# Moving a row normalisation from ScalarE to VectorE in a planned MLP, attention and MLP kernel, with new planner numbers

## The reference, cut to what matters

```
x = x + 0.5 * ffn(layernorm(x))     # pass 0
x = x + attn(layernorm(x))          # pass 1 (projections), pass 2 (output projection)
x = x + 0.5 * ffn(layernorm(x))     # pass 3
layernorm(x) = (x - mean) / sqrt(var + eps)
ffn:  fp4-quantise rows by blocks of 16 -> gate, up (704 wide) -> silu(gate) * up
      -> fp4-quantise -> down (256 wide)
attn: q, k, v projections; rms norm and rotary on q, k; 16 half-heads, causal softmax;
      difference of the two halves with lambda; layer norm per head; output projection
```

## Time and profile before

| | us |
|---|---|
| three runs, median | 2178.94 |
| three runs, lowest and highest | 2178.08 to 2182.39 |
| the profiled execution, device time | 2177.42 |
| its span, first to last instruction | 2175.7 |
| mean granted TensorE clock, share of full | 0.975 |

### The profile page before, as it was taken

The page is one execution under the profiler, slowest core; times in us unless marked ns, Lnnn a source line. Parts: engine busy times, 40 slices in busy tenths (PEclk is TensorE's granted clock), DMA queues, the critical chain, the costliest instruction groups (busy, mean ns, idle before and its releaser), DMA issues. The chain is left out here.

```text
span 2175.7 us, 39394 instructions
## 1 busy us (share of the span) xinstructions
PE 1884.4 (87%) x13634; PEld 782.7 (36%) x13634; DVE 1566.9 (72%) x3324; ACT 1710.4 (79%) x2531; POOL 1365.6 (63%) x1439
## 2 busy tenths in 40 slices
PE   2677998898998988998899899899998889999966
PEld 1333433343432433343332343343432333432223
DVE  7898888677826878887743998888864678741365
ACT  3456787977889888878889898778888889789952
POOL 7797776566724776886743686866853667630255
PEclk9899999999999999999999999999999999999987
DMA  4134544324211444334221445232441343320013
GB/s 124 31 60 79 88 72 85 51 63 86 42 40 27 84 84 94 68 70 84 47 52 20 69 78 89 59 91 49 64 70 37 62 81 68 74 47 1 11 33 69
DMA packets 477493, 136.16 MB, mean 63 GB/s; under 512 B 458224, under 2 KB 477040, under 8 KB 477296
## 3 DMA queue, kind: packets, MB, share of 16 engines
q1 hardware_dynamic: 477296, 133.65, 33.0%
HBM read 11.96 MB, written 8.39 MB: 9 GB/s over the span
## 5 line engine op out<-in xcount | busy, mean ns | idle before, releaser
L1048 ACT ACTIVATE probs<-psum 128x1024 f32<-128x1024 f32 (+3 forms) x1280 | 1066.9, 922 | 94.6 <-PE psum L1333 79.3
L1351 PE MATMUL psum_o<-probs,v_sb 128*32 128x512 f32 (+3 forms) x5120 | 570.5, 542 | 20.0 <-POOL probs L954 7.8
L1296 PE MATMUL psum<-w_gu_T,xT 128*128 128x512 f16 (+1 forms) x2304 | 510.8, 371 | 60.9 <-DMA xT<-x 14.6
L1333 PE MATMUL psum<-q_stack,k_stack 64*128 64x512 f16 (+3 forms) x2560 | 388.3, 353 | 84.4 <-ACT probs L1048 65.5
L1296 PEld LDWEIGHTS psum<-w_gu_T,xT 128*128 128x128 f16 x2304 | 213.7, 99 | 330.1 <-issue 50.1
L954 POOL TENSOR_SCALAR_AFFINE_SELECT probs<-probs 128x512 f32<-128x512 f32 x256 | 180.0, 709 | 237.4 <-ACT probs L1048 236.3
L1309 PE MATMUL psum<-w_down_T,hT 128*128 128x256 f16 x2176 | 267.8, 279 | 41.1 <-DMA hT<-h 19.7
L1333 PEld LDWEIGHTS psum<-q_stack,k_stack 64*128 64x128 f16 x2560 | 99.5, 93 | 503.6 <-ACT probs L1048 396.7
L921 POOL TENSOR_TENSOR hq<-grid,qscale 128x704 f32<-128x704 f32 x128 | 179.6, 1404 | 113.8 <-DVE grid L1147 113.8
L928 POOL TENSOR_TENSOR h<-hq,h 128x704 f16<-128x704 f32 x128 | 203.2, 1587 | 73.8 <-ACT h L1004 73.5
L1309 PEld LDWEIGHTS psum<-w_down_T,hT 128*128 128x128 f16 x2176 | 208.7, 100 | 106.7 <-issue 36.5
(11 more groups left out here) (120 smaller groups left out, 2294.6 us busy)
## 6 DMA issues: line engine op xcount, KB each, us to landing
xb<-L_attn_x SPq DMA_DIRECT2D x16, 512.0 KB, 3.9
out<-xb SPq DMA_DIRECT2D x16, 512.0 KB, 3.0
xT<-x SPq DMA_TRANSPOSE x128, 3.1
hT<-h SPq DMA_TRANSPOSE x128, 3.5
k_stack<-st SPq DMA_TRANSPOSE x64, 3.3
q_stack<-st SPq DMA_TRANSPOSE x64, 3.3
k_stack<-L_ffn_w_down SPq DMA_DIRECT2D x1, 704.0 KB, 4.0
k_stack<-L_ffn_w_gate SPq DMA_DIRECT2D x1, 512.0 KB, 5.1
```

Source lines behind the costliest of these rows:

```text
L1048: nc.scalar.activation(probs[:, s % 3, 2 * u:2 * u + 2, q0:CHUNK], psum[:, plan.pairs[s, u]:plan.pairs[s, u] + 2, q0:CHUNK], ACT.Exp, scal ...
L1296: last = nc.tensor.matmul(bank(e)[:, 0:hi - lo], xs[:, x, t % 2, k, :], w_gu_T[:, w, k, lo:hi], start=n == 0, stop=n == len(parts) - 1)
L1333: last = nc.tensor.matmul(psum[:, plan.pairs[s, u] + j, q0:CHUNK], k_stack[half, at, h, kt % NTC * P:(kt % NTC + 1) * P], q_stack[half, c ...
L1351: last = nc.tensor.matmul(psum_o[at:at + VD, q0:CHUNK], v_sb[:, kt // NTC % SLOTS * NTC + kt % NTC, 2 * g + u, :], probs[:, s % 3, 2 * u + ...
```

## The change

The normalisation stage `norm_a` is issued by DVE: one `tensor_scalar` for each tile computes `(x - mean) * rstd` with mean and `rstd` as scalars per partition. ACT no longer has the stage. POOL's `rstd` ends with `rstd` itself; the two instructions for `offset`, the tile and two semaphores are gone. In the hand-placed beginning DVE runs `norm_a` right before `scale_x`, and ACT runs nothing between its second and third weight square. The planner's tables change: `COST`, `REACH`, `DRAIN` and landing times, a new `LATE` and `AFTER` for hand-over times of single pairs of stages, `EARLY` for a bank that comes free before its stage ends, and the time that issuing a transposing DMA holds SP. `DUE` has new values in all its families and `WIDE` another selection. The diff, without the numbers of `DUE` and some declarations:

```
-WIDE = {0: (2, 3, 4, 8, 13, 14, 15), 1: (3, 7, 11, 12, 14, 15), 2: (1, 3, 4, 5, 7, 11, 14, 15), 3: (0, 2, 3, 4, 6, 7, 11, 14, 15)}
+WIDE = {0: (1, 5, 8, 9, 10, 12, 13, 14, 15), 1: (0, 1, 2, 3, 5, 6, 7, 13, 14, 15), 2: (3, 6, 8, 9, 11, 13, 14, 15), 3: (1, 5, 7, 10, 11, 13, 14, 15)}
-LANDING = 4000
+LANDING = 3400
...
-COST = dict(load=100, store=100, add_down=460, add_out=470, copy_o=670, dequant_h=1380, dequant_x=1060, divide_h=1390,
-            divide_x=1060, down=1970, gate=720, grid_h=890, grid_x=680, head_stats=2750, heads_out=2080, head_sum=460, square_o=400,
-            hidden=1380, high_h=800, high_qk=1160, high_x=640, low_h=1520, low_qk=1160, low_x=1160,
-            mask=630, norm_a=1090, norm_heads=690, norm_qk=680, points_h=890, points_x=690,
-            project_out=690, project_qk=1360, project_v=690, quant_h=1650, read_qk=690,
-            read_v=480, rms=4050, rope=1930, rope_add=1270, rstd=3340, scale_x=1290, square_h=790,
-            square_x=620, stats=1820, tanh=700, transpose_o=590, turn_x=200, turn_h=200, turn_qk=200)
+COST = dict(load=700, store=700, add_down=475, add_out=475, copy_o=680, dequant_h=1385, dequant_x=1058, divide_h=1385,
+            divide_x=1056, down=1860, gate=690, grid_h=890, grid_x=685, head_stats=2870, heads_out=2010, head_sum=460, square_o=400,
+            hidden=1300, high_h=790, high_qk=1150, high_x=625, low_h=1522, low_qk=1158, low_x=1156,
+            mask=640, norm_a=540, norm_heads=690, norm_qk=685, points_h=890, points_x=690,
+            project_out=650, project_qk=1300, project_v=650, quant_h=1650, read_qk=690,
+            read_v=470, rms=4170, rope=1940, rope_add=1270, rstd=2780, scale_x=1295, square_h=795,
+            square_x=620, stats=1820, tanh=690, transpose_o=470, turn_x=1250, turn_h=1400, turn_qk=2700)
 OVERLAP = dict(tensor=0, vector=80, scalar=100, gpsimd=40, sync=0)
-REACH = dict(tensor=140, vector=40, scalar=40, gpsimd=80, sync=100)
+REACH = dict(tensor=60, vector=40, scalar=40, gpsimd=80, sync=100)
 RELEASE = 60
-DRAIN = 140
+DRAIN = 170
+LATE = {("rstd", "norm_a"): 55, ("high_qk", "low_qk"): 60, ("copy_o", "transpose_o"): 85, ("scores", "exp"): 60}
+AFTER = {("grid_h", "points_h"): 35, ("grid_x", "points_x"): 35, ("gate", "gate"): 100, ("gate", "quant_h"): 100,
+         ("add_out", "stats"): 90, ("add_down", "stats"): 90, ("head_sum", "head_stats"): 90,
+         ("head_stats", "norm_heads"): 35, ("rope", "rms"): 35, ("norm_a", "scale_x"): 35}
+EARLY = dict(quant_h=460, scale_x=390)
...
-            dequant_h=0, low_h=0, rope_add=0, low_qk=0, mask=0)
+            dequant_h=0, low_h=0, rope_add=0, low_qk=0, mask=0, norm_a=0)
-TURNED_X, TURNED_H = 3300, 4200
+TURNED_X, TURNED_H, TURNED_QK = 2200, 2400, 2200
...
+        def lag(m, n):
+            of, to = self.stages[m][0], self.stages[n][0]
+            pair = m[0], n[0]
+            return REACH[to] + LATE.get(pair, 0) if of != to else AFTER.get(pair)
...
-                    met[n] = max(end[m] + REACH[self.stages[n][0]] if self.stages[m][0] != self.stages[n][0] else
-                                 left[m] for m in self.stages[n][3])
+                    met[n] = max(left[m] if lag(m, n) is None else end[m] + lag(m, n) for m in self.stages[n][3])
...
-                    loans[loan] = free_bank[b] = end[name] + REACH["tensor"]
+                    loans[loan] = free_bank[b] = end[name] + REACH["tensor"] - EARLY.get(name[0], 0)
...
-            add(norm, "scalar", at("norm_a"), needs, takes, frees)
+            add(norm, "vector", at("norm_a"), needs, takes, frees)
...
-                add(norm, "scalar", of_pair("norm_a", *pair), [("rstd", 1, c), ("norm_heads", "x", 2, NTC * (c - 2) // 2 - 1) if c >= 3 else None],
+                add(norm, "vector", of_pair("norm_a", *pair), [("rstd", 1, c), ("norm_heads", "x", 2, NTC * (c - 2) // 2 - 1) if c >= 3 else None],
...
-                [], [("st", t)], lands=LANDING)
+                [], [("st", t)], lands=TURNED_QK)
...
-                    [("scores", (s, u))], weight=230 * full // CHUNK)
+                    [("scores", (s, u))], weight=4 + 215 * full // CHUNK)
...
-                    weight=170 + 855 * full // CHUNK)
+                    weight=150 + 855 * full // CHUNK)
...
-                [("psum_o", (c, g))], [("probs", s)], weight=900 * full // CHUNK)
+                [("psum_o", (c, g))], [("probs", s)], weight=25 + 860 * full // CHUNK)
...
-                    n, o = EARLY_RSTD[e], offset[:, slot, :]
-                    nc.gpsimd.tensor_scalar(o, mean_var[:, slot, :, 0], -1.0, None, ALU.mult)\
-                        .then_inc(mean_negated, 1)
-                    nc.gpsimd.tensor_tensor(rstd[:, slot, :], t, y, ALU.mult).then_inc(early_rstd, 1)
-                    pool.wait_ge(mean_negated, n + 1)
-                    pool.wait_ge(early_rstd, n + 1)
-                    nc.gpsimd.tensor_tensor(o, o, rstd[:, slot, :], ALU.mult).then_inc(rstd_ready, 1)
+                    nc.gpsimd.tensor_tensor(rstd[:, slot, :], t, y, ALU.mult).then_inc(rstd_ready, 1)
...
-                elif e[0] == "norm_a":
...
-                    act.wait_ge(rstd_ready, RSTD["rstd", pas, 2 * p // NTC] + 1)
-                    for j in range(2):
-                        t = 2 * p + j
-                        i = t % NTC
-                        last = nc.scalar.activation(a[:, j * C:(j + 1) * C], xb[:, t % XB, :], ACT.Identity,
-                                                    bias=offset[:, slot, i:i + 1], scale=rstd[:, slot, i:i + 1])
-                    last.then_inc(early_normed, 1)
...
+                elif e[0] == "norm_a":
...
+                    before = last_low("x", (pas, p))
+                    if before:
+                        dve.wait_ge(low_ready, before)
+                    dve.wait_ge(rstd_ready, RSTD["rstd", pas, 2 * p // NTC] + 1)
+                    for j in range(2):
+                        t = 2 * p + j
+                        i = t % NTC
+                        last = nc.vector.tensor_scalar(a[:, j * C:(j + 1) * C], xb[:, t % XB, :],
+                                                       mean_var[:, slot, i, 0:1], rstd[:, slot, i:i + 1],
+                                                       ALU.subtract, ALU.mult)
+                    last.then_inc(early_normed, 1)
...
-                    vector_stages(dve, first["scale_x"])
+                    vector_stages(dve, first["norm_a"] + first["scale_x"])
...
-                        if i == 2:
-                            scalar_stages(act, first["norm_a"])
```

More of the change, by code:

```diff
@@ new lines @@
+    "quant_h3": (1257700, 128329, -1198020, -1930392, -197546, -2299546, -263471, 155916, 2507493, 4447889, -819760, -668114, -238246, 1056057, 2572883, 58971, 2588350, 2016998, 3140457, 1006166, -1192775, -432802, 3693548, 2754134, 3822575, 5763425, 6796468, 3720783, 5866866, 9472418, 2713345, 6331789),
+    "read_qk": (-2275201, -1665241, 46619, 1209385, -486133, 28992, -1106356, 346919, -1856335, -806712, 3076828, 3141783, 2439936, 4170447, 1363555, 1134917, 1057196, 2240352, 4011510, 4859110, 3179162, 5012717, 395203, 2114656, 2012872, 4693511, 650673, 2763797, -978070, 633382, 2104505, 3508172),
@@ new lines @@
+    "read_v": (-1738083, 193962, 648071, 1421781, 968234, 378105, 227935, 1835047, 1238024, 2157734, 688980, 1032469, 3935987, 6100348, -1588094, -177118, 1648812, 3826205, 2259728, 4995974, 2003981, 2282527, -359172, 2828252, 302645, 2071181, 1519232, 3276594, 2212377, 3332822, 632515, 2142383),
+    "rms": (-1424270, 382061, -1056880, 242518, 1329166, 1655857, -427873, 383003, 1198440, 2019739, -108322, -65278, 4240380, 5265659, -1848729, -1525625, 2689322, 4127738, 1532729, 3294075, 3363210, 4343741, -1217088, -61745, 3413416, 4800902, 219235, 2263829, -545703, 676159, -674618, 345017),
@@ L636, in macaron_kernel @@
         root_t = sb("root_t", [P, NTC])
-        offset = sb("offset", [P, STATS, NTC])
         minus_half = sb("minus_half", [P, NTC])
@@ L730, in macaron_kernel @@
         QUANT = ordinals(order["vector"], ("quant_h", "scale_x"))
-        EARLY_NORM = ordinals(order["scalar"], ("norm_a",))
-        EARLY_RSTD = ordinals(order["gpsimd"], ("rstd",))
+        EARLY_NORM = ordinals(order["vector"], ("norm_a",))
         DIVIDE = ordinals(order["gpsimd"], ("divide_x", "divide_h"))
@@ L978, in scalar_stages @@
                         .then_inc(full(e)[0] if e[1] == "x" else square_done, 1)
-                elif e[0] == "norm_a":
-                    pas, p = e[2:]
-                    slot = STAT[pas, 2 * p // NTC] % STATS
-                    a = buffers("x", (pas, p))[0]
-                    before = last_low("x", (pas, p))
-                    if before:
-                        act.wait_ge(low_ready, before)
-                    act.wait_ge(rstd_ready, RSTD["rstd", pas, 2 * p // NTC] + 1)
-                    for j in range(2):
-                        t = 2 * p + j
-                        i = t % NTC
```

(9 more changed lines are left out.)

61 lines of the change are left out of this document (28 added, 33 removed), and 136 rows, old and new, of the table DUE.

## The result

The changed kernel takes 2159.86 us in the median (2157.39 to 2161.51, 4 runs) against 2178.51 (2171.99 to 2182.39) for the kernel before, measured beside it: ratio 0.9916, 95% interval 0.989 to 0.9943. It is faster by 0.84%, about 19 us; forecast were 73. The range of 2050 to 2186 held the time, the forecast's own range of 2075 to 2145 did not.

A forecast was written before the change was run, and what follows sets the result against it. The kernel was taken to be bound by hand-overs between nearly balanced engines. Terms of -52, -2, -1.7, +13 and -30 us summed to -73, from 2177.4 to 2104.7, predicted as a 2106 us median; range 2050 to 2186, 8 in 10.

The forecast's parts named there:

- the worth of ACT's relief, -52 us: ACT loses norm_a: 139 us of its time come free, worth 0.37 each on the path; range 24 to 104 us.
- VectorE's side, +13 us: DVE gains 86 us of norms and holds, less 59.2 us of waits; net 27, costing in 11 of 22 stretches.
- The first rival: Each of 192 DVE norms is held by POOL through the shared port, 0.5 us each; slower, 2198 us; chance 0.12.
- a mean over 0.6 us speaks for the port: Sign in the norms' group on DVE: a mean this long would support the first rival; expected median was near 278 ns.
- The order's term, -30 us: New order from corrected transposing-DMA times removes a quarter of 122 us of transfer and loading waits; range 0 to 61.
- the 122 us of DMA waits of the prediction: Waits before the change: 76.6 us for transposing transfers in five entries, plus 45.4 us of DVE waiting for loaded rows.
- POOL's -2: POOL loses the offset's two instructions, 23.6 us of busy time; with 1 of the chain's 13, worth 2 us.
- the setup's -1.7: In the setup POOL's weight scaling can begin up to 1.65 us earlier, counted as 1.7 us.
- everything counts: Rival: ACT is nearly always last, its 104 us come off in full; 2040 to 2075 us; chance 0.14.
- PE is the bound: Rival: PE at about 90% needs that time, ACT's time is hidden; terms -24, +13, -4, -5; 2159 us; chance 0.22.
- if PE's waits for exps don't fall below 345 us and the time falls, the order did it: Sign on PE's waits for exps, 396.7 us before: it credits any gain to the new order.
- The sign of being wrong: Prediction wrong if PE's idle time doesn't shrink by about 70 us, or DVE's rstd waits grow past 30.8 us.

The follow-up runs named there:

- the second order: New table, norm left on ScalarE, due times from a search carried on for 40 minutes more, against the kernel before: 0.9831 (2138.49 us).
- the first refit: New table, norm left on ScalarE, due times fitted anew by a search of 75 minutes, against the kernel before: 0.9849 (2143.05 us).
- The other two orders with the norm on VectorE: The changed kernel with due times refitted from its own, 1.0002; and refitted with 660 ns a norm pair in the table, 0.9967; both against the kernel before.

## Why the prediction was wrong

**The step that failed is the worth of ACT's relief, -52 us.** The prediction divided the 396.7 us that PE waits for exps by the 1066.9 us of exps and took the 0.37 as the price of any ACT time. The runs price it at 0.10 in the old order and 0.21 in a fitted one. ACT lost 84 us of busy time where the prediction counted 103.9, and put 35.4 us of waits on top of it; at these prices the 84 are worth 8 to 18 us, and what the waits are worth wasn't measured. A wait's total says how often an engine was the last to arrive, not what happens when it arrives earlier: the freed ACT waits for PE (80.7 to 143.6 us), and PE, which the prediction wanted to free, brought nothing when it was relieved.

**The second is VectorE's side, +13 us.** The norm alone was estimated at 278 ns and measures 328. The holds were put at 0.34 us for one norm of a pair, 33 us; measured are 152.4 - 192 x 0.328 = 89 us, or 83 by the 0.72 us of the free pair, because both norms of a pair can be held. The relief by 59.2 us of waits was counted against it; the fitted order with the norm on ScalarE has most of that relief too. DVE gained 121 us, not 86, and taking the holds away is worth 36 us on the path. The first rival had this mechanism right, and nearly its size: 0.43 to 0.47 us for each norm (83 or 89 / 192) where it said 0.5, beyond the 0.31 from which it was to decide. What kept it from deciding the sign is the order, which it took to gain nothing. By the prediction's own signs, a mean over 0.6 us speaks for the port: it is 0.841.

**The order's term, -30 us, came out in size; its cause is not shown.** The new table with a fitted order and nothing moved gives (1 - 0.9849) x 2177 = 33 us, 37 in the second order. Whether the corrected table or merely another search made them isn't separated: no run refits the old table with the norm on ScalarE, though with the norm on VectorE the old table, refitted, stayed at 1.0307. Nor are waits for transfers shown to be the cause: the 122 us of DMA waits of the prediction are 75.7 in the changed kernel, where the five entries on transposes come to 46.6 us and the rows' loading to 29.1, and 82.8 in the first refit, which is faster. The fall in DVE's wait for the norms, 37 us, belongs to the same term.

**The sum, mended:** -33 to -37 for table and order, and for the move, by subtraction, +15 (0.9916 - 0.9849) against the first refit and +19 against the second, where the prediction had -52 -2 -1.7 +13 = -43. With ACT's relief at -8 to -18, this leaves +23 to +37 for VectorE's side, about what the holds measured. The other two orders with the norm on VectorE put the move higher, at 26 to 37 us, and with the old table it costs 67 (1.0307): table and move don't simply add, so the split holds for the new table alone. POOL's -2 and the setup's -1.7 are too small for these runs; POOL's time is worth 0.25, so its 14 us less (1365.6 to 1351.2) may be worth 3.6, an estimate from that row.

**The rivals.** That everything counts fell with ACT's price. That PE is the bound gave 2159 for a measured 2159.86, by a mechanism that the run with less PE work refutes: its ACT, DVE and order terms (-24, +13, -5) were each wrong and added up right. Of the signs named, the one that told the cause from the trace alone was this: if PE's waits for exps don't fall below 345 us and the time falls, the order did it. They stand at 374.1. The sign of being wrong came true as well: PE's idle time shrank by 12 us, not by 70.

## What to carry to other kernels

The price of an engine's time is a run that takes a little of its work away with the order kept; neither its busy share nor the total of the waits for it gives that price, and the fuller engine can be worth the less: ACT at 79% a tenth, POOL at 63% a quarter. Where an order is fitted to durations, a change and a refit must be priced with each part refitted by itself: undoing one part under the other's order showed losses of 74 and 180 us, where refits gave a gain of 33 and a loss of 67. A planned length ranks two arrangements only if the table has the right price for what differs between them. Before work moves to VectorE, price the very form of the instruction beside a busy POOL, for 2 columns were held nearly as long as 256.

## What the hardware showed that was not expected

With POOL's queue full, one norm gets through for each POOL instruction, and POOL hardly pays. The twelve multiplications beside the 16 norms took

```profile
12.65 20.08 POOL L44 TENSOR_TENSOR pc<-pa,pb 128x704 f32<-128x704 f32 x12 [9.43 <-DVE dst L77]
...
123.08 19.55 POOL L44 TENSOR_TENSOR pc<-pa,pb 128x704 f32<-128x704 f32 x12 [6.45 <-DVE dst L107]
```

1.67 us each beside the norms, and 1.63 beside the form with a sum, which is not held. So the engine that comes to wait is VectorE: a held norm takes 1.67 us, five times its time alone, for 3% of POOL's. And the form with a second output, which gives up the multiplication, is the cheaper one beside POOL, 0.41 against 1.67 us, while alone it takes 0.08 us more than the norm's 0.33.
